# First stage of a graph kernel: moments, guesses and refined deviations made one unit further ahead of the normalising

## The reference

```
x = x + _L0_gnn_ref(_layernorm(x), src, dst, edge_weight, W1, b1, W2, b2)   # support = layernorm(x) @ W1, gathered per edge, summed per node
x = x + _L0_ffn_ref(_layernorm(x), ...)      # 6 experts, the best 2 mixed
x = x + _L1_gnn_ref(_layernorm(x), edge_attr_256, ...)
x = x + _L1_ffn_ref(_layernorm(x), ...)      # 8 experts, the best 2
_layernorm(x) = (x - mean) / sqrt(var + 1e-05)
```

## Time and profile before

| | |
|---|---|
| time of three runs, median (lowest to highest) | 4262.16 us (4260.17 to 4264.4) |
| time of the profiled execution | 4256.23 us |
| its span from the first to the last instruction | 4254.5 us |
| end of the first stage (last store issued; the next stage's first DVE operation) | 79.8 us; 83.40 us |
| PE busy in 0 to 83.4 us | 47.61 us |
| DVE busy in 0 to 83.4 us | 48.16 us |
| ACT busy in 0 to 83.4 us | 44.37 us |
| mean granted clock of PE in 0 to 83.4 us, as a share of full speed | 0.88 |

### The profile page before, as it was taken

One profiled execution on the slowest core, in us unless ns is written; L12 is line 12 of the kernel. 1 busy time (PEld: TensorE's weight loads), 2 busy tenths in 40 slices (PEclk: granted clock), 3 DMA queues, 4 the chain that ended last, 5 costly groups with the idle time before them and its releaser, 6 DMA issues. The chain is left out here.

```text
span 4254.5 us, 68494 instructions
## 1 busy us (share of the span) xinstructions
PE 3499.8 (82%) x17723; PEld 3081.8 (72%) x17723; DVE 2292.7 (54%) x7003; ACT 1939.1 (46%) x3024; POOL 2806.6 (66%) x2732
## 2 busy tenths in 40 slices
PE   5777777877747999999999968888887887649999
PEld 5666666666636888888888867777777777538887
DVE  5566656565543455555445436666666666632222
ACT  4555555555531333333333445555555555423333
POOL 3677777777767777766666137777777777354334
PEclk8888888888867999999999977777777777559999
DMA  5555555555552222222222136666666666544443
GB/s 145 177 187 184 176 180 178 184 177 178 179 166 57 65 66 72 65 63 68 65 64 64 31 113 214 205 209 209 209 209 202 214 210 187 172 142 88 97 99 60
DMA packets 275818, 599.12 MB, mean 141 GB/s; under 512 B 61759, under 2 KB 150558, under 8 KB 275499
## 3 DMA queue, kind: packets, MB, share of 16 engines
q1 hardware_dynamic: 153243, 334.71, 24.4%
q0 software_dynamic: 115808, 248.88, 21.8%
q10 hardware_dynamic: 6576, 13.36, 0.9%
HBM read 460.33 MB, written 138.24 MB: 141 GB/s over the span
## 5 line engine op out<-in xcount | busy, mean ns | idle before, releaser
L1656 POOL DMA_INDIRECT y_node<-node_table,src_sb x832 | 850.8, 1023 | 382.5 <-issue 380.6
L494 POOL DMA_INDIRECT conv_gath<-support_table,src_sb x832 | 875.9, 1053 | 269.2 <-issue 256.3
L1096 POOL DMA_INDIRECT x_gath<-hidden_table,src_sb x832 | 795.4, 956 | 361.8 <-issue 260.1
L649 PE MATMUL conv_pz<-conv_we,conv_edge 128*128 128x256 f32 x2240 | 631.0, 445 | 69.8 <-PEq L97 69.7
L1669 PE MATMUL y_pa<-y_hot,y_node 128*128 128x64 f32 x3328 | 518.1, 323 | 192.8 <-PEq L97 192.1
L1669 PEld LDWEIGHTS y_pa<-y_hot,y_node 128*128 128x128 f32 x3328 | 500.9, 237 | 226.0 <-issue 223.1
L649 PEld LDWEIGHTS conv_pz<-conv_we,conv_edge 128*128 128x128 f32 x2240 | 502.0, 230 | 159.6 <-issue 74.4
L640 PE MATMUL conv_ps<-conv_hot,conv_gath 128*128 128x64 f32 x1664 | 258.0, 307 | 214.4 <-DMA conv_gath<-support_table,src_sb 212.2
L640 PEld LDWEIGHTS conv_ps<-conv_hot,conv_gath 128*128 128x128 f32 x1664 | 244.9, 221 | 247.0 <-DMA conv_gath<-support_table,src_sb 240.1
L1721 ACT ACTIVATE y_node<-y_node 128x1024 f32<-128x1024 f32 x208 | 219.3, 1055 | 344.2 <-ACTq L97 343.6
L1679 PE MATMUL y_pz<-y_we,y_edge 128*128 128x256 f32 x1104 | 360.8, 498 | 11.9 <-PEq L97 11.9
(11 more groups left out here) (257 smaller groups left out, 5817.2 us busy)
## 6 DMA issues: line engine op xcount, KB each, us to landing
conv_edge<-in_edge_t SPq DMA_DIRECT2D x140, 512.0 KB
edge_mish_table<-conv_neg SPq DMA_DIRECT2D x140, 512.0 KB
y_neg<-edge_mish_table SPq DMA_DIRECT2D x139, 512.0 KB, 4.1
y_edge<-in_edge_t SPq DMA_DIRECT2D x69, 512.0 KB
e_rows<-expert_rows SPq DMA_DIRECT2D x56, 272.0 KB, 3.4
conv_gath<-support_table,src_sb POOLq DMA_INDIRECT x832
x_gath<-hidden_table,src_sb POOLq DMA_INDIRECT x832
y_node<-node_table,src_sb POOLq DMA_INDIRECT x832
```

Source lines behind the costliest of these rows:

```text
L494: pool.indirect_dma_start(gath[g % SLOTS][:, j, :], None, table[:, :], bass.IndirectOffsetOnAxis(ap=c.src[:, col:col + 1], axis=0),).then_ ...
L649: last = pe.matmul(ps_z[r % 2][:, j, :], edge[r][:, m, j * P:(j + 1) * P], we[:, m, :], start=m == 0, stop=m == KD - 1)
L1096: pool.indirect_dma_start(gath[g % SLOTS][:, j, :], None, table[:, :], bass.IndirectOffsetOnAxis(ap=c.src[:, col:col + 1], axis=0),).then_ ...
L1656: pool.indirect_dma_start(node[g % SLOTS][:, j, :], None, c.t3[:, :], bass.IndirectOffsetOnAxis(ap=c.src[:, col:col + 1], axis=0),).then_i ...
```

## The change

In units, DVE's lead over the normalising grows by one. Before the loop DVE now makes moments 0, 1 and 2 and refines 0 and 1. In iteration u of the loop it refines unit u + 2 first and then makes the moments of u + 3; before, it made the moments of u + 2 and then refined u + 1. ACT guesses unit u + 3 instead of u + 2 in iteration u, and does so after `evacuated(u)` instead of ahead of it. `refined(u)` has one more wait, on `xn_ready`: shift[u % 2] must have been read by `spread(u - 2)` before it is written. No operation is added or removed; PE, POOL and SP keep their lists.

```diff
             def refined(u):
                 dve.wait_ge(guess_ready, u + 1)
+                if u >= 2:
+                    dve.wait_ge(xn_ready, u - 1)
                 refine_deviation(nc, c, chain, guess[u % 2], work, shift[u % 2], *UNITS[u]).then_inc(rstd_ready, 1)
...
             moments(0)
             moments(1)
             refined(0)
+            moments(2)
+            refined(1)
             for u in range(U):
                 if u == 2:
                     spans()
                 if u == U - 4:
                     relative()
                 if u + 2 < U:
-                    moments(u + 2)
-                if u + 1 < U:
-                    refined(u + 1)
+                    refined(u + 2)
+                if u + 3 < U:
+                    moments(u + 3)
                 if u:
                     copied(u - 1)
             copied(U - 1)
...
             guessed(0)
             guessed(1)
             spread(0)
+            guessed(2)
             for u in range(U):
                 if u + 1 < U:
                     spread(u + 1)
-                if u + 2 < U:
-                    guessed(u + 2)
                 evacuated(u)
+                if u + 3 < U:
+                    guessed(u + 3)
```

## The result

| | before | changed |
|---|---|---|
| median of the runs timed together (lowest to highest) | 4262.16 us (4255.54 to 4266.43, 5 runs) | 4236.23 us (4233.16 to 4243.64, 5 runs) |
| profiled execution, its span | 4256.23 us, 4254.5 us | 4236.68 us, 4234.9 us |
| next stage's first DVE operation | 83.40 us | 66.98 us |

The changed kernel is 25.9 us faster, ratio 0.9942 with a 95% interval of 0.9927 to 0.9956. 16.2 us had been forecast (4246.0, range 4239 to 4254).

What follows compares the result with a forecast made beforehand. It took waits in a DVE, ACT, PE ring to bound the first stage, with ACT's 3.45 us a unit as the new bound. Gains 1.5 + 12.15 + 2.6 = 16.2 us off 4262.16 gave 4246.0, range 4239 to 4254.

Steps and rivals of the forecast that it cites:

- What bounds, and the ring: First stage: DVE copy, moments, refining, ACT normalising and PE product wait on each other in a loop, 5.09 us a unit.
- Middle, 12.15 us: First stage, units 4 to 11: seven steps take 24.15 us instead of 36.3, so 12.15 gained, the main term.
- ACT's 3.45 a unit: First stage, new order: ACT's own work, 3.40 + 0.05 us a unit, is the longest and becomes the bound.
- Beginning, 1.5 us: First stage up to unit 4: its normalising starts at 26.2 instead of 27.69 us, 1.5 gained.
- End, 2.6 us: First stage from unit 11's normalising: last copy ends 12.3 us after its start instead of 14.94, 2.6 gained.
- The clock: PE in the first stage: granted clock taken to stay high; rival that it goes on falling, 4248.6 to 4252, chance 0.17.
- The sign named for it: Changed kernel's timeline, first stage: PE's granted clock is 1.00 from 27 to 60 us.
- the 4252 case: PE's clock goes on falling in the first stage, every other stretch low: 6 us lost; clock rival's chance 0.17.
- it moves as a block, and so do all later stages, because the barrier lets nothing past: After the first stage's last copy: store, landing, barrier and later stages only start earlier, by the 16.2 us gained.
- the added wait on `xn_ready` I cost at nothing: DVE's `refined(u)`: the new wait has always been met, cost 0; at a 0.05 us handover DVE reaches 3.23, below 3.45.
- The one on later stages: Rival: stage gain stays, but later stages differ by as much as runs do; total gain 0 to 8, 4254 to 4262; chance 0.11, shared with DVE's list binding.
- PE's wait for `b_xn` falls under 18: First stage sign: PE's wait for the normalised rows falls from 30.3 us to under 18.

## Why the prediction was wrong, by its own steps

- **What bounds, and the ring.** Right. With DVE's order alone the ring opens, with ACT's alone it stays.
- **Middle, 12.15 us.** Measured 36.30 - 24.01 = 12.29. ACT's 3.45 a unit was 3.43 in the mean: 3.30 where nothing held it up, with three longer steps.
- **Beginning, 1.5 us.** Unit 4 starts at 25.45, not 26.2: 2.2 gained. 0.8 of it is that x came earlier in that execution (unit 2's moments at 9.84 instead of 10.64), and that differs between profiles (9.69 to 10.64 in the old order); the 1.4 left are the forecast's 1.5.
- **End, 2.6 us.** The last copy ends at 62.29, 12.83 behind unit 11's start instead of 12.3: 2.1 gained. The three terms: 16.6 measured, 16.2 forecast; from stage to stage 16.4, and by the stages alone 16.2.
- **The clock.** Right on the side taken: it stays at the high level in 46.00 to 60.10. The sign named for it, 1.00 in all of 27 to 60 us, was missed in the first profile (0.51 in 28.00 to 31.50) and met in the second. The rule of the Trainium skill (TensorE: Matmul & The Clock Gate, Part 4: PE-mode transpose), by which transposes do not count as matmuls do and which had the 4252 case, did not come to bear: a third of PE's blocks were transposes there and the level held. No run here has transposes alone, so the rule itself is not tested.
- **The step that failed** is in the sum: "it moves as a block, and so do all later stages, because the barrier lets nothing past", with "the added wait on `xn_ready` I cost at nothing". The wait does cost nothing where it stands (alone, its stage ended within 0.8 us of before). But it makes DVE's list 12 instructions longer, and with just that length the second stage's loop runs 8.3 us shorter. The new order without it measured 4246.43 us, where 4246.0 was forecast for the change; that it comes so near is in part luck, since its interval is 5 us wide to either side.
- **The rivals.** The one on later stages gave them the wrong sign and called them chance; they differ by chance from execution to execution (1158.1 to 1165.9 within one class) and by class besides. The range was built from the first stage alone, and reached 7 us below the forecast.
- **"PE's wait for `b_xn` falls under 18"** missed: 21.1 us, of which 9.9 is the wait for the first unit.

What stays open: how twelve instructions shift DVE's loop against POOL's gathers. That the number acts through their meetings is shown; why 12 and 13 do and 0, 6, 15 and 28 don't is not, and no larger period was tried. The kept traces hold one sign of it. At the end of each round of the second stage's loop on DVE, from the last semaphore instruction to the loop's branch, 0.27 us pass in all seven profiles with 12 or 13 more instructions ahead (the one with L514 cut among them) and 0.147 us in the eleven others, in each of the last 29 rounds. In the two with 15 more a stop of the same size (0.17 us instead of 0.03) stands near the beginning of the round instead, behind a register load. So DVE stops for 0.12 to 0.14 us at a place that depends on how many instructions stand ahead; that this stop is what changes the meetings is not shown.

8.3 us are located, as a difference of means over sixteen profiles. In the third stage the same means differ by 1.5 us, behind it by nothing. The two profiles each of before and changed kernel alone would not show it: their second stages differ by 3.2 us in the mean, their third ones by 5.8. The third stage lasted 1256.3 to 1258.7 us in four of the six profiles with DVE's new order and 1259.0 to 1263.9 in the other two and in all of the old order; no run takes that apart. DVE's order alone came out at 4234.65 us though its first stage is 3.3 us longer than the changed kernel's; its later stages' sum was the shortest of the sixteen profiles, and no run says why.

## What to carry to other kernels

A ring in which a product's copy-out stands ahead of the next units' preparation on the same in-order engine is opened by moving the preparation one unit ahead; the gain is the old pace less the new one, which the work of the busiest engine sets, times the number of units (5.19 less 3.43, times 7, here). Before a gain or loss of a few tenths of a per cent is put down to an edit, time the same kernel with the instruction count restored: here 12 instructions that do nothing were worth 0.28% and 6, 15 or 28 nothing. Where POOL's gathers pace a stage, look for long DVE operations beside them, those with two SBUF inputs first; that cost (54 us under L514 in this kernel's second stage, and 33 more at L510, which has one) is larger than either part of this change.

## What the runs showed of the hardware that was not expected

- Twelve or thirteen waiting instructions on DVE ahead of a loop changed that loop's stage by 8.3 us of 1168.6 (0.7%, means of six and ten profiles); the same number on ACT or behind the loop did not. With them 0.27 us instead of 0.147 pass on DVE at the end of each round of the loop.
- A gather on POOL that begins during a 1.22 us two-input DVE operation, but for its last 0.12 us, takes 1.4 to 1.53 us instead of 0.94 and ends 0.82 us after it; under an operation of the same length with one input in PSUM it takes 0.94. Without the two-input operation's work, 832 gathers took 809.3 us instead of 875.9.
